# State space loop of a perceiver kernel: half of the C products on GpSimd, summed in pairs, and two reorderings ahead of the last attention

## The reference, cut to what matters

```
xc    = silu(conv_b + sum_k xpad[:, k:k+l] * conv_w[:, k])            # 512 channels
dbc   = xc @ W_x.T ;  dt, Bm, Cm = 128, 16 and 16 columns of it
delta = softplus(dt @ W_dt.T + b_dt) ; A = -exp(A_log)                # 16 states
dA    = exp(delta * A) ;  dBx = delta * Bm * xc
h_t   = dA_t * h_(t-1) + dBx_t                                        # over 128 steps
y     = sum_s hs[s] * Cm[s] + xc * Dp ;  out = (y * silu(z)) @ W_out.T
...
q, k, v = 16 heads of 16, each quantised to 8 bits (q, k per row, v per column)
attn    = softmax(q k^T over 4096 keys), quantised to 0..255 ; out = attn v @ Wp + bp
```

## Time and profile before

| | us |
|---|---|
| median of 3 runs (440.26 to 444.31) | 444.06 |
| the profiled execution, its own time | 442.38 |
| its span, first to last instruction | 440.6 |

### The profile page before, as it was taken

How to read it: one execution, slowest core, us unless ns; L and a number is a source line. 1 busy time by engine, 2 the same in 40 slices (tenths; PEclk the granted TensorE clock), 3 DMA queues, 4 the chain that set the end, 5 groups by cost and what they waited for, 6 DMA issues and landing times.

```text
span 440.6 us, 9345 instructions
## 1 busy us (share of the span) xinstructions
PE 408.4 (93%) x3822; PEld 297.9 (68%) x3822; DVE 357.3 (81%) x582; ACT 303.0 (69%) x382; POOL 105.3 (24%) x177
## 2 busy tenths in 40 slices
PE   8989899999999999999789999999999999888897
PEld 4878778855555554576347777777777777755686
DVE  2846662879999999987899999999999999654343
ACT  3245834788888776553789999999999999811110
POOL 3100402044444444001245333321111111100000
PEclk9999999999999999999989999999999999889899
DMA  7898912411001100369488789999999894300000
GB/s 281 295 425 301 196 70 73 192 32 31 25 27 27 31 3 0 140 227 438 210 243 249 251 274 263 243 255 251 250 220 311 203 273 101 51 1 0 1 1 24
DMA packets 48245, 71.46 MB, mean 162 GB/s; under 512 B 38954, under 2 KB 41674, under 8 KB 42698
## 3 DMA queue, kind: packets, MB, share of 16 engines
q1 hardware_dynamic: 47626, 67.32, 51.4%
q0 software_dynamic: 576, 3.54, 2.1%
HBM read 61.58 MB, written 1.15 MB: 142 GB/s over the span
## 4 chain that ended last, share of the span: by engine, by line
PE 43%; DVE 41%; issue 7%; ACT 4%; DMA 3%; SPq 1%; DVEq 0%; ACTq 0%
DVE arena L1387 20%; DVE w L1387 9%; PE ps L1671 6%; PE ps L1781 5%; PE ps L1680 5%; PE ps L2058 4%; DVE arena L1398 3%; PE ps L1564 2%; PE ps L1628 2%; DMA arena<-in_segg 2%; PE ps L1720 2%; PE ps L2069 2%; PE ps L1588 1%; PE ps L1493 1%; PE ps L1837 1%
## 5 line engine op out<-in xcount | busy, mean ns | idle before, releaser
L1387 DVE CUSTOM_DVE_ANT_0 arena<-ps,arena 128x1024 f32<-128x1024 f32 x88 | 107.5, 1277 | 0.1
L1897 PE MATMUL ps<-arena 128*128 128x512 bf16 x256 | 77.6, 384 | 11.0 <-DVE arena L1387 7.4
L1002 ACT ACTIVATE arena<-arena 128x4096 uint8<-128x4096 f32 x21 | 78.0, 3716 | 7.8 <-POOL arena L697 7.8
L1921 PEld LDWEIGHTS ps<-cst,arena 128*128 128x128 f32 x384 | 48.2, 144 | 23.2 <-ACT arena L1002 7.2
L1921 PE MATMUL ps<-cst,arena 128*128 128x128 f32 x384 | 59.8, 280 | 2.7 <-ACT arena L1017 2.1
L1941 PE MATMUL ps<-vrow,arena 128*128 128x16 f16 x806 | 52.6, 170 | 0.5 <-ACT w L1017 0.5
L1941 PEld LDWEIGHTS ps<-vrow,arena 128*128 128x128 f16 x806 | 49.2, 96 | 3.9 <-ACT w L1017 0.6
L1387 DVE CUSTOM_DVE_ANT_0 w<-ps,arena 128x1024 f32<-128x1024 f32 x40 | 49.6, 1276 | 0.0
L1944 PE MATMUL ps<-vrow,arena 128*128 128x16 f16 x768 | 45.8, 170 | 0.0
L672 POOL TENSOR_TENSOR arena<-arena 128x1024 f32<-128x1024 f32 x14 | 33.0, 2358 | 39.2 <-DVE arena L1276 39.2
L1944 PEld LDWEIGHTS ps<-vrow,arena 128*128 128x128 f16 x768 | 40.9, 98 | 1.4 <-DVE arena L1398 0.3
(11 more groups left out here) (278 smaller groups left out, 743.8 us busy)
## 6 DMA issues: line engine op xcount, KB each, us to landing
arena<-ks_scr SPq DMA_DIRECT2D x32, 1024.0 KB, 5.6
arena<-in_w SPq DMA_DIRECT2D x1, 4488.0 KB, 22.1
arena<-in_columns SPq DMA_DIRECT2D x4, 1024.0 KB, 7.8
arena<-in_w0b SPq DMA_DIRECT2D x1, 2560.0 KB, 16.7
w<-in_w SPq DMA_DIRECT2D x1, 2286.0 KB, 10.8
arena<-in_w SPq DMA_DIRECT2D x1, 2048.0 KB, 7.7
arena<-in_fill SPq DMA_DIRECT2D x1, 2048.0 KB, 9.1
arena<-bc_scr SPq DMA_DIRECT2D x14, 128.0 KB, 3.0
```

Source lines behind the costliest of these rows:

```text
L1002: act.activation(out8[:, :, 0], s_sb[u % 3], ACT.Exp, bias=nb[:, u % 3:u % 3 + 1], accum_out=zall[:, u:u + 1]).then_inc(p_ready, 1)
L1387: dve.tensor_tensor_reduce(s_sb[slot][:, keys], ps[:, 2 * (c % 2):2 * (c % 2) + 2, :].rearrange("p a n -> p (a n)"), ksb[h % 2][:, keys], ...
L1897: mm = pe.matmul(bank(2 * (c % 2) + m, 0, 512), qz[h // 8][:, h % 8, b * L:(b + 1) * L], kT[:, h // 8, k:k + 512], start=True, stop=True)
L1921: mm = pe.transpose(bank(4 + n % 3, k * P, P), words[:, w:w + P], ident)
```

## The change

The product of the second state of a step, hst[1] * C, moves from VectorE to GpSimd (`second_product`) for steps 0 to 6. GpSimd reads the row of C from SBUF (`bcc`, two buffers), where the SP queue fetches it, as it does rows of B. The products go to `hp`, three buffers in the space of an array that is dead by then, and in steps 1, 3 and 5 GpSimd adds two of them (`pair_of`); TensorE sums one tensor for each pair (`sum_of_pair`) and the product of step 6 alone. In step 7 VectorE makes both products. `scan(i, 1)` waits for GpSimd's product of the step before; `input_of` waits one scan less; the scales come behind the new product on GpSimd; `largest` moves ahead of `scaled_keys` on VectorE. TensorE's `read_rows` broadcasts one row in place of two.

In the last attention chunk 0 is evicted by VectorE in every second unit in place of two of three. ScalarE's dummy exponential moves ahead of `columns(3, 0)`, and TensorE's `queries(1)` ahead of `value_rows(2)` and `query_columns(0)`.

```diff
-    return (u % 3 < 2 or u >= LAST - 1) if c == 0 else ((u == LAST - 1 and c < TURNED) or (u == LAST and c < 3))
+    return (u % 2 == 0 or u >= LAST - 1) if c == 0 else ((u == LAST - 1 and c < TURNED) or (u == LAST and c < 3))
+def products(i):
+    return 3 * (i // 2) + i % 2 + 1
...
+        hp = early[:, 0:3 * ET * T].rearrange("k (s t n) -> k s t n", s=3, t=ET)
+        bcc = early[:, 3 * ET * T:3 * ET * T + 2 * T].rearrange("k (s n) -> k s n", s=2)
...
@@ SP queue, inputs(n)
+                if n % 2:
+                    i = (n - 3) // 2
+                    if i >= 2:
+                        sp.wait_ge(hp_made, products(i - 2))
+                    sp.dma_start(bcc[:, i % 2, :], bc_scr[2 * i + 1:2 * i + 2, 1, :].partition_broadcast(P).rearrange("p o t -> p (o t)"))\
+                      .then_inc(ld_b[n % 4], 16)
@@ GpSimd
-                pool.wait_ge(ld_b[n % 4], 16 * ((n + 2) // 4))
-                pool.wait_ge(h_ready, 2 * i)
+                pool.wait_ge(ld_b[n % 4], 16 * (1 + s) * ((n + 2) // 4))
+                pool.wait_ge(h_ready, max(2, 2 * i - 1 + s))
...
+            def second_product(i):
+                n = 2 * i + 3
+                pool.wait_ge(ld_b[n % 4], 32 * ((n + 2) // 4))
+                pool.wait_ge(h_ready, 2 * i + 2)
+                if i >= 3:
+                    if i % 2:
+                        pool.wait_ge(hp_used, (i - 3) // 2 + 1)
+                    else:
+                        pool.wait_ge(hp_made, 3 * ((i - 4) // 2) + 3)
+                pool.tensor_tensor(hp[:, i % 3], hst[:, 1, :].rearrange("p (t n) -> p t n", t=ET),
+                                   bcc[:, i % 2, :].unsqueeze(1).broadcast_to([P, ET, T]), ALU.mult).then_inc(hp_made, 1)
+            def pair_of(p):
+                a, b = hp[:, (2 * p) % 3], hp[:, (2 * p + 1) % 3]
+                pool.wait_ge(hp_made, 3 * p + 2)
+                pool.tensor_tensor(a, a, b, ALU.add).then_inc(hp_made, 1)
...
                 input_of(i + 1, 0)
+                second_product(i)
                 if i + 2 < NC:
                     scales_of(i + 2)
                 input_of(i + 1, 1)
+                if i % 2:
+                    pair_of(i // 2)
@@ ScalarE
+            act.activation(spare[:, :], spare[:, :], ACT.Exp)
             columns(3, 0)
-            act.activation(spare[:, :], spare[:, :], ACT.Exp)
@@ VectorE, scan(i, s)
                 if i:
-                    dve.wait_ge(hc_made, 2 * i - 1 + s)
+                    if s == 0:
+                        dve.wait_ge(hc_made, i)
+                    else:
+                        dve.wait_ge(hp_made, products(i - 1))
@@ VectorE, a step
                 read_out(i, 0)
+                if i == NC - 1:
+                    read_out(i, 1)
                 if i + 2 < NC:
                     key_maxima(i + 2)
-                read_out(i, 1)
+                largest(i)
                 if i + 2 < NC:
                     scaled_keys(i + 2)
-                largest(i)
@@ TensorE
-                for s in range(2):
+                for s in range(2 if i == NC - 1 else 1):
...
+            def sum_of_pair(p):
+                pe.wait_ge(hp_made, products(6) if p == 3 else 3 * p + 3)
+                summed(hp[:, (2 * p) % 3]).then_inc(hp_used, 1)
...
-                sum_of(i, 0).then_inc(hc_used[0], 1)
-                sum_of(i, 1).then_inc(hc_used[1], 1)
+                if i and i % 2 == 0:
+                    sum_of_pair(i // 2 - 1)
+                sum_of(i)
...
             columns(3, 1)
+            queries(1)
+            query_columns(0)
             value_rows(2)
-            query_columns(0)
-            queries(1)
```

More of the change, by code:

```diff
@@ L347, in perceiver_kernel @@
         pe_step = sem("pe_step")
-        (QLAT, WABS, MLAT, LAST_TAPS, DLAT, DLIN0, DLIN1, DBC, B_ROWS, Q_PS0, Q_TR0, Q_PS1, Q_TR1, ON_TR0, ON_TR1, VALUE0_MADE, Q_MADE,
+        (QLAT, WABS, MLAT, LAST_TAPS, DLAT, DLIN0, DLIN1, DBC, B_ROWS, Q_PS0, Q_PS1, Q_TR0, Q_TR1, ON_TR0, ON_TR1, VALUE0_MADE, Q_MADE,
          KEYS_MADE, VALUES_MADE, OA_TR0, OA_TR1, LOGITS) = range(1, 23)
@@ L411, in perceiver_kernel @@
         h_ready = sem("h_ready")
-        hc_used = [sem(f"hc_used{k}") for k in range(2)]
+        hc_used = sem("hc_used")
+        hp_made = sem("hp_made")
+        hp_used = sem("hp_used")
         th_done = sem("th_done")
@@ L1281, in read_out @@
                 dve.wait_ge(h_ready, 2 * i + s + 1)
[L1282 to L1285, removed]
+                if s == 0:
+                    if i:
+                        dve.wait_ge(hc_used, i)
+                    else:
+                        dve.wait_ge(skip_read, 1)
                 dve.wait_ge(c_ps, i + 1)
@@ L1768, in read_rows @@
                 if i:
-                    pe.wait_ge(hc_made, 2 * i)
-                for s in range(2):
+                    pe.wait_ge(hc_made, i)
+                for s in range(2 if i == NC - 1 else 1):
                     n = DS + 2 * i + s
@@ L1774, in read_rows, with summed, sum_of @@
                 mm.then_inc(c_ps, 1)
-            def sum_of(i, s):
-                pe.wait_ge(hc_made, 2 * i + s + 1)
-                rows = hc[:, s].rearrange("p t n -> p (t n)")
+            def summed(rows):
                 for n in range(2):
-                    mm = pe.matmul(bank(6 + n, 0, 512), ident, rows[:, n * 512:(n + 1) * 512],
+                    mm = pe.matmul(bank(6 + n, 0, 512), ident, rows.rearrange("p t n -> p (t n)")[:, n * 512:(n + 1) * 512],
                                    start=False, stop=True, skip_group_check=True)
                 return mm
+            def sum_of(i):
+                pe.wait_ge(hc_made, i + 1)
+                summed(hc[:, 0]).then_inc(hc_used, 1)
+            def sum_of_pair(p):
+                pe.wait_ge(hp_made, products(6) if p == 3 else 3 * p + 3)
+                summed(hp[:, (2 * p) % 3]).then_inc(hp_used, 1)
             keys(2)
@@ L1804, in _ @@
             awake(18, 1)
-            sum_of(NC - 1, 0)
-            pe.wait_ge(hc_made, 2 * NC)
+            sum_of_pair(3)
+            sum_of(NC - 1)
+            pe.wait_ge(hc_made, NC + 1)
             for n in range(2):
```

## The result

The changed kernel takes **452.77 us** (median of 4 executions, 448.61 to 453.95) against 444.19 for the kernel before beside it (4 executions, 440.26 to 445.43): ratio 1.019, 95% interval 1.010 to 1.028, which lies wholly above 1. Slower, as forecast, and inside the range; the forecast number, 456.5, is 3.7 us too high. The profiled execution of after took 453.95 us with a span of 452.1, that of before 442.38 with 440.6.

A forecast was written before the change was run, and what follows sets the result against it. No one engine bounds the span; in the state loop VectorE and TensorE are always busy, in the attention VectorE never rests. +15.1 + 1.0 - 1.1 - 2.5 = +12.5 us on 442.38 gives 454.9, stated as 456.5 for the median; range 451 to 464.

The forecast's parts named there:

- What bounds the kernel: No one engine bounds the whole span; in the state loop a scan and a GpSimd product exclude each other, first come first served.
- (a): Rival, faster: scans and GpSimd's products overlap freely in the loop, steps bound by TensorE's 10.1 us; about 434 us; 7%.
- (b): Rival, about even: only a scan that comes second waits, a product runs on; loop -2 to +5, kernel 438 to 446; 5%.
- Part 1, the loop: State loop: scans and GpSimd's work stand in one line, steps 11.6 us, or 13.9 with a pair addition; +15.1 us.
- the upper bound of 19.0: State loop: +19.0 us if each of the 14 handovers between scans and GpSimd costs 0.14 us instead of overlapping.
- the 1.8 us more: State loop: 7 x 0.25 us longer by the skill page, where the blocked party goes on some 115 ns after VectorE's end.
- The covers: State loop: C-row fetches cost nothing; reciprocal and scaling, waiting for late scales, end at 6.7 us, inside GpSimd's 7.3.
- Part 2, TensorE's clock: TensorE falling to 1.2 GHz in the loop (late keys, 2.3 us each time) or output projection behind (1.7); 0 to +7, taken +1.
- rival (c): Slower still: clock falls in the loop and keys come late, or handovers cost; no eviction gain; 462 to 468 us; 18%.
- Part 3: Before the attention: table load and queries(1) moved ahead, VectorE's second quantising starts sooner; -1.1 us, bounds 0 and -1.5.
- Part 4: Attention: VectorE's evictions in units below 30 fall from 20 to 15, ScalarE has room; -2.5 us, bounds 0 and -3.0.
- The sum: Whole kernel: +12.5 us on the profiled 442.38 gives 454.9; that execution lies 1.7 below the median, so 456.5.

The follow-up runs named there:

- experiment 3: Changed kernel, scan's second operand from PSUM from step 1 on (wrong numbers), with a wait for TensorE's C row: 442.74 us, ratio to before 1.000.
- experiment 4: Changed kernel with only the added wait of the scan for TensorE's C row, operands in SBUF as they were: 451.12 us, ratio 1.026.
- experiment 6: Kernel before with only the moved first input, which may start after the first scan instead of both: 440.26 us, ratio 1.000.
- experiment 2: Changed kernel with the state loop's part alone, attention as before: 453.96 us against 440.95, ratio 1.032.
- experiment 1: Kernel before with only the three edits around the attention (evictions, table load, order of queries): 436.64 us against 440.95, ratio 0.988.
- experiment 7: Kernel before with only the two reorderings (table load and queries(1) moved): 438.32 us against 440.17, ratio 0.996.
- experiment 8: Kernel before with only five evictions moved from VectorE to ScalarE: 437.76 us against 440.17, ratio 0.997.
- experiment 5: Changed kernel without the pair additions, TensorE summing each of GpSimd's products by itself: 444.81 us, ratio 1.010.

## Why the prediction was right, step by step

**What bounds the kernel: right.** That scan and product exclude each other rested on one scan of 3.683 us and two casts; experiments 3, 4 and 6 show it, with the scan's second operand as the switch. Rivals (a) and (b) fall: with the operands as they are, no scan runs beside a product or a pair addition, whichever comes second.

**Part 1, the loop: +15.1 forecast, +14.05 measured.** The steps were to last 11.6 and 13.9; they last 11.5 and 13.63. The start and step 1 came as forecast (11.7 us from GpSimd's first input to the end of the scans). Of the later steps two short ones are 0.1 less each and three long ones 0.27: -1.0. The long steps' share is a miscount of mine: I gave every step two handovers of 0.14, but where a pair addition falls the engines alternate and there are four, 4.46 + 9.75 - 4 x 0.14 = 13.65. Step 7 came as forecast (11.18 against 11.2). That a handover overlaps, and does not cost, held wherever the second instruction had been issued and stood; only the last scan, issued when its input was done (184.20 + 4.33 = 188.53), began 0.13 behind it (188.66). The case behind the upper bound of 19.0 did not occur, nor did the 1.8 us more that the prediction sets against its own sum. The covers held too: no second product shows a wait for its C row, and the reciprocal's wait for the late scales, 1.52 us, hides beside GpSimd's work.

**Part 2, TensorE's clock: +1, and it held for the wrong reason.** Falls inside the loop came, in steps 1 and 6, but cost nothing: I had let late keys push VectorE's path by 2.3 us, when VectorE has over 1.5 us of waiting left in a step that GpSimd bounds (the 1.52 ahead of the reciprocal; the 1.35 for the keys took its place). All five profiles with the new loop have falls in it, 3.4 to 13.6 us in all, and none of the five with the old loop has one; yet the loop took 92.73, 92.74 and 92.84 us with 10.2, 13.6 and 10.2 us of them (after, experiments 2 and 4). So the new loop lowers the mean granted clock without costing time by that. The +2.19 that the ledger shows sits at the attention's end, where TensorE is at half speed for 13.65 us against 6.83 in before's profile. That is not the change's: the same stretch, from the last maxima to the first addition, takes 14.05 in before, 16.18 and 16.27 in the profiles of experiments 1 and 7, 14.12 and 14.07 in 8 and 6, and 12.41 and 14.06 in experiments 2 and 4, which have the whole new loop. As far as one profile of each can show, it varies with the execution. Taking it out leaves +9.4 for the change (-0.41 + 14.05 - 1.06 - 3.20), and the one execution of after with the highest clock (0.992), 448.61, lies 9.5 over the 439.1 of before at 0.99 and above. The -0.41 is scatter too: the first scan starts between 98.15 and 99.67 in the other profiles. So rival (c), slower still by the clock, has no support in these profiles. That +1 for the clock lay so near to the +2.19 of the profile is luck.

**Part 3: -1.1 forecast, -1.06 measured**, -1.07 alone: VectorE's wait of 1.30 became 0.24.

**Part 4: -2.5 forecast, -3.2 measured** in after, and with the same edit on the kernel before -2.5 alone and -2.4 with the reorderings. The maxima take 163.29 to 164.24 us in five profiles with the new evictions and 166.26 to 167.09 in the four with the old ones, 2.8 apart in the mean: nearly all of the 3.0 us was kept, not part of it. ScalarE did have the room. The exception is experiment 3, told there. The longer group of maxima in after, in experiment 8 and in experiment 1 (page rows: busy us, mean ns, idle before and for what):

```profile
L1429 DVE CUSTOM_DVE_ANT_0 arena<-ps,arena 128x1024 f32<-128x1024 f32 x88 | 107.4, 1271 | 0.0
```

```profile
L1387 DVE CUSTOM_DVE_ANT_0 arena<-ps,arena 128x1024 f32<-128x1024 f32 x88 | 107.5, 1272 | 0.7 <-issue 0.6
```

```profile
L1387 DVE CUSTOM_DVE_ANT_0 arena<-ps,arena 128x1024 f32<-128x1024 f32 x88 | 107.6, 1279 | 0.5 <-ACT arena L1002 0.5
```

VectorE never waited in after; in the other two it stood for 0.7 and 0.5 us, once for ScalarE's exponential, as I had feared for all profiles. The new loop alone does not keep them away: with it and the same evictions the maxima take 163.51 us in experiment 4 without a wait, but 164.24 in experiment 5, where VectorE stood for 0.8. So part of the -3.2 of after is scatter between executions. The loop alone leaves this stretch as it was: 166.26 in experiment 2.

**The sum.** On the profiled execution's own time: 454.9 forecast, 453.95 measured; -1.05 is the loop, -0.7 the evictions, -0.4 the start, +1.2 the clock. The remaining distance of 456.5 is the step to the median: I added 1.7 because before's profiled execution lay below its median, and after's lies 1.2 above.

## What to carry to other kernels

Before moving work from VectorE to GpSimd, look at how many operands of VectorE's instructions lie in SBUF. Beside the read-outs, with one, GpSimd's work here was free; against the scans, with two, the two engines' times add up, so sum them first. With the scan's second operand in PSUM, in a variant that computes other numbers, the loop was 9.4 us shorter, as much as the whole change lost. In a trace, an instruction that is longer than its peers and ends its own usual time behind the end of another engine's is a wait in disguise. And a change of several parts is to be taken apart before it is dropped: here the loop's part loses some 13 us (14.06 in its stretch), and three small edits beside it win 4.3.

## What the runs showed that I had not expected

- A handover between the two engines does not cost where the second instruction has been issued and stands: it starts 0.13 to 0.2 us before the first is shown to end, so alternating more often makes the sum slightly shorter (13.63 us for a step of 14.21 us of instructions). One that is issued only when the first is done began 0.13 us behind it.
- TensorE at 1.2 GHz for 10.2 us inside the loop moved no end of a step, and 13.65 us of it at the attention's end made that stretch longer by 2.2 to 3.8 us (16.24 against 14.05 with half as much of it, and 12.41 with none).
